# Attention tiles paired: one DMA transpose for two query tiles, another tile order, other places in the written order

## The chip, the cores and the metric

The kernel runs on one core of a Trainium2 chip. The metric is device time in microseconds (us), the median of several runs. The core has five engines with queues of their own: PE (matrix products), DVE (vector), ACT (scalar), POOL (GpSimd) and SP, which here only issues DMAs.

## The reference, cut to what matters

One transformer layer over x of 2 x 1024 tokens with 512 features: x = x + layernorm(attention(layernorm(x))), then x = x + layernorm(ffn(layernorm(x))). The attention has 32 heads with a compressed latent:

```
q      = rms_norm(x @ wq_a.T, q_norm_w) @ wq_b.T        # 32 heads of 128 + 64 (rotary)
kv     = x @ wkv_a.T                                    # latent of 64, rotary key of 64
kv_up  = rms_norm(kv[:64], kv_norm_w) @ wkv_b.T         # k_nope, v of each head
scores = (q_nope . k_nope + q_pe . k_pe) * scale        # causal mask
out    = softmax(scores) @ v ;  return out @ wo.T
```

The feed-forward part is silu(x @ w_gate) * (x @ w_up) @ w_down with a hidden width of 1376.

## The kernel before

Keys are folded into the queries' weights, so each head's query and key have 128 rows: 64 latent and 64 rotary. Both batches and 32 heads make 64 heads, worked one after the other. A head has eight query tiles of 128 queries; tile j sees (j + 1) x 128 keys, since the mask is causal. A job is one tile of one head, and there are 512 jobs (`NJ`), in the order of `TILES` within each head. Values are the latent itself, split into a high and a low fp16 half (`lat2`).

What a job goes through:

- scores (PE): fp32 split into high and low fp32r halves, three products (high x high, high x low, low x high) for each chunk of up to 512 keys, into one of four PSUM slots `s_ps` (`NS`, widths in banks in `SLOTS`). It waits for `q_split`, POOL's count of prepared 512-query halves, and for `p_low` of four jobs before.
- minimum (DVE, L1354): adds the mask and finds the row's extreme, whose value is read out by a second small instruction. exponential (ACT, L1152). split_high (ACT, L1159) and split_low (DVE, L1367): the probabilities as two fp16 halves in `pk`, a ring of `NPK` buffers.
- turn_probs (SP, L760): a DMA transpose from `pk` to `pt`, a ring of `NPT` buffers. It moves 2(j + 1) blocks of 128 x 128.
- values (PE, L972), once for two jobs: one matmul for each block into `o_ps`, whose column 128 is the sum of the row. invert_sums (DVE), outputs_norm (ACT, L1168, two instructions), outputs_add (POOL, L1561, once for four jobs), outputs_turn (PE, L980, four transposes once for four tiles of two heads), outputs_high (ACT), outputs_low (DVE).

Beside that run the queries of the next head in two halves (c = 0, 1): queries (PE, five matmuls of 512 columns into the bank `x_ps`), queries_raw (ACT, L1142, drains the bank), queries_swap (SP, L770, two DMAs that swap the rotary rows into `qs`), and queries_turn (POOL, L1531 to L1544, five instructions, the last of which writes q_low). Further, output (PE, 12 matmuls of 512 columns a head on average) multiplies four heads' outputs with folded weights, and fold_values prepares these in the first 32 heads. `x_ps` is one bank for queries, fold_values, outputs_turn and output, each of which waits until the one before it was drained.

Nothing is scheduled at run time. `attention_order` gives every piece of work a step on a common scale, one step for each job, and sorts them; each engine's program is the sorted list, cut to what that engine does. A step says only in which order an engine meets its work; the time follows from semaphores. `AFTER_SCORES`, `VALUES`, `AFTER_VALUES`, `TURN_STEPS`, `Q_STEPS` and the others are these distances: queries(n, c) stands at step 8(n - 1) + `Q_STEPS[c]`, values(u) at 2u + 1 + `VALUES`, and each list of AFTER is added to the step of the work that it is named for. Pieces with one step keep the order in which they were added, scores first. `prologue_order` does the same for the first stage (latents, folded weights), and `feed_forward_order` lets token and weight preparation advance by `pace` pieces beside each gate and up product. From `EARLY_START` on, pieces of the feed-forward part are laid between the last steps of attention.

Of the kernel before, what the change touches and what calls it, by code (L numbers as in the profile page):

```python
# [11 lines left out]
P = 128  # L12
# [23 lines left out]
NX, NA, NPK, NPT, NON = 4, 3, 4, 6, 8  # L36

SLOTS = (2, 1, 1, 2)
# [4 lines left out]
AFTER_SCORES = dict(minimum=0.86, exponential=0.73, split_high=1.39, split_low=2.35,  # L43
                    turn_probs=2.29)
VALUES = 6.15
AFTER_VALUES = dict(invert_sums=1.03, outputs_norm=0.4, outputs_add=2.09)
TURN_STEPS = (3.09, 3.21)
AFTER_TURN = dict(outputs_high=0.2, outputs_low=0.82)
Q_STEPS = (0.06, 2.46)
AFTER_QUERIES = dict(queries_raw=0.0, queries_swap=0.0, queries_turn=1.54)  # L50
O_STEPS = (3.53, 6.77)
AFTER_OUTPUT = dict(output_add=0.72, output_store=1.5)
FOLD_STEP = 1.04
AFTER_FOLD = dict(fold_high=0.0, fold_low=1.09, fold_store=1.5)
END_STEP = 7.5


AFTER_TILE = dict(x_load=-2.13, statistics=-0.35, deviation=-0.05, normalise=0.74, transpose_x=1.38,
                  x_high=1.56, x_low=2.15, project=3.23, squares=3.26, norm_keys=4.28, halves=5.02,
                  norm_queries=5.02, transpose_latents=5.91, latents_high=6.09, latents_low=6.62)  # L60
FOLD_FROM, FOLD_EVERY, LOAD_AFTER = 3.28, 2.2, 0.49
AFTER_WEIGHTS = dict(rotary=-0.29, weights_high=0.2, weights_low=0.84, fold_out=1.6)
FIRST_QUERIES = 0.18
TABLES_STEP = 6.94
EARLY_START = 1
# [12 lines left out]
TILES = [6, 1, 3, 7, 4, 0, 2, 5]  # L78
PLACE = [TILES.index(j) for j in range(JT)]
JOBS = [(n, j) for n in range(NHEADS) for j in TILES]  # L80
# [161 lines left out]
class Memory:  # L242
# [64 lines left out]
    def attention(self, ctx, sb, pb):  # L307
        self.m_in = sb(ctx, "m_in", [P, 2, GK, 2, DM], F32R)
        self.nbias = sb(ctx, "nbias", [P, 4])
        self.rinv = sb(ctx, "rinv", [P, NON])  # L310
        self.pk = sb(ctx, "pk", [P, NPK, 2 * SEQ], F16)
        self.pt = sb(ctx, "pt", [P, NPT, 2 * JT, P], F16)
        self.o_norm = sb(ctx, "o_norm", [P, NON, P])
        self.o_pair = sb(ctx, "o_pair", [P, 2, 4, P])
        self.ot_high = sb(ctx, "ot_high", [P, 2, GK, SEQ], F32R)
        self.ot_low = sb(ctx, "ot_low", [P, 2, GK, SEQ], F32R)
        self.acc = sb(ctx, "acc", [P, JT, DM])
        self.s_ps = [pb(ctx, f"s_ps{i}", n * CW) for i, n in enumerate(SLOTS)]
# [54 lines left out]
    def halves_of(self, i):  # L373

        width = (JOBS[i][1] + 1) * P
        return self.pk[:, i % NPK, 0:2 * width].rearrange("p (t h s) -> p t h s", h=2, s=P)
# [13 lines left out]
def prologue_order():  # L390
# [28 lines left out]
def attention_order(end):  # L419
# [15 lines left out]
    for u in range(NJ // 2):  # L435
        step = 2 * u + 1 + VALUES
# [132 lines left out]
def feed_forward_order():  # L569
# [117 lines left out]
def sync_program(e, M, S, D):  # L687
# [174 lines left out]
def tensor_program(e, M, S):  # L862
# [85 lines left out]
    def scores(i):  # L948
# [7 lines left out]
        for c, width in halves(j):  # L956
            keys = slice(b * SEQ + c, b * SEQ + c + width)
            ins = chain(e, s[:, c:c + width], three(M.q_high[:, r, q], M.q_low[:, r, q],
                                                M.k_high[:, keys], M.k_low[:, keys]))
        ins.then_inc(S.s_mm)  # L960

    def values(u):
        w.wait_ge(S.ident, 3)
        for i in (2 * u, 2 * u + 1):
            n, j = JOBS[i]
            b = HEADS[n][0]
            w.wait_ge(S.turned[i % NPK], DMA * (i // NPK + 1))
            if u:
                w.wait_ge(S.o_norm, u)
            blocks = range(2 * (j + 1))  # L970
# [109 lines left out]
def scalar_program(e, M, S):  # L1080
# [602 lines left out]
```

## Time and profile before

| | |
|---|---|
| median of 3 runs | 1831.28 us (1829.5 to 1832.15) |
| the profiled execution | 1834.6 us, span 1832.8 us |
| PE busy over the span | 1593.2 us (87%), 10720 matmuls |
| DVE, ACT, POOL busy | 1132.7, 1102.4, 951.7 us |
| mean granted TensorE clock | 0.96 |
| DMA transposes | 512, median 3.9 us from issue to landing |
| stages | latents to about 100 us, attention to about 1370, feed-forward to the end |

The span runs from the first to the last instruction; the execution's own time has some time around it. Engines' busy times overlap, so they don't add up to the span. In the profile L105 is the line of a helper that issues chains of matmuls; its groups are told apart by their tiles. A matmul's duration is longer than the distance to the next one's start, because they are pipelined. `SPq` rows are issues of DMAs on SP's queue.

### The profile page before, as it was taken

Reading aid. Unit: us, or ns where it says so; the run is one execution under the profiler, and the core shown is the slowest. Engines: PE = TensorE matmul, PEld = TensorE weight load, DVE = VectorE, ACT = ScalarE, POOL = GpSimd, SP = SyncE. Lnnn points to the kernel's source line nnn. Section 1 sums busy time; section 2 is a strip of 40 time slices with the busy share of each in tenths; the row PEclk is TensorE's granted clock in tenths of the full one; section 3 lists DMA queues with packets and bytes.
Section 4 is the critical chain, followed back from the end, with each engine's and each line's share of the span. In section 5 each row is a group of like instructions: output and inputs, shape, how many; then the busy total and the mean of one; then the engine's idle time right before and its main releaser. Section 6 shows DMA issues by size and latency. Waiting matters only on the chain. (4 is left out here: it accounts for less than half of the span.)

```text
span 1832.8 us, 30900 instructions
## 1 busy us (share of the span) xinstructions
PE 1593.2 (87%) x10720; PEld 1326.1 (72%) x10720; DVE 1132.7 (62%) x2548; ACT 1102.4 (60%) x2159; POOL 951.7 (52%) x911
## 2 busy tenths in 40 slices
PE   5877888989888888988989889888986889999986
PEld 5766776767777777777877777777775667888765
DVE  7856666767676767766767767676765453323355
ACT  5666776767676767767877767677762433312121
POOL 2655765666666656665766766666641232111132
PEclk9989999999999999999999999999997899999998
DMA  8668898989879988998889788888985500201022
GB/s 294 223 121 181 167 187 150 181 152 176 183 151 187 172 167 156 196 172 181 166 170 174 149 168 148 162 166 155 181 143 189 188 27 20 69 0 37 0 81 81
DMA packets 669291, 268.91 MB, mean 147 GB/s; under 512 B 616624, under 2 KB 627376, under 8 KB 666960
## 3 DMA queue, kind: packets, MB, share of 16 engines
q1 hardware_dynamic: 669136, 266.93, 68.8%
q8 instruction: 86, 1.41, 0.3%
q14 instruction: 69, 0.57, 0.1%
HBM read 69.70 MB, written 29.36 MB: 54 GB/s over the span
## 5 line engine op out<-in xcount | busy, mean ns | idle before, releaser
L1354 DVE CUSTOM_DVE_ANT_0 s_ps<-s_ps,far_sb 128x896 f32<-128x896 f32 (+7 forms) x512 | 388.2, 758 | 136.0 <-PE s_ps L105 135.3
L1367 DVE SCALAR_TENSOR_TENSOR pk<-s_ps,pk 128x896 f16<-128x896 f32 (+7 forms) x512 | 384.2, 750 | 115.4 <-ACT pk L1159 114.6
L1159 ACT ACTIVATE pk<-s_ps 128x896 f16<-128x896 f32 (+7 forms) x512 | 333.0, 650 | 91.4 <-DMA pt<-pk 79.9
L1152 ACT ACTIVATE s_ps<-s_ps,nbias 128x896 f32<-128x896 f32 (+7 forms) x512 | 367.5, 718 | 20.6 <-DVE nbias L1354 16.5
L105 PE MATMUL s_ps<-k_high,q_high 128*128 128x512 f32 (+3 forms) x768 | 289.6, 377 | 82.3 <-POOL q_low L1544 69.6
L972 PE MATMUL o_ps<-lat,pt 128*128 128x130 f16 x4608 | 317.6, 223 | 6.9 <-ACT o_norm L1168 3.6
L972 PEld LDWEIGHTS o_ps<-lat,pt 128*128 128x128 f16 x4608 | 271.7, 99 | 45.7 <-issue 31.5
L105 PE MATMUL s_ps<-k_low,q_high 128*128 128x512 f32 (+3 forms) x768 | 272.2, 354 | 0.0
L105 PE MATMUL s_ps<-k_high,q_low 128*128 128x512 f32 (+3 forms) x768 | 271.6, 354 | 0.0
L1531 POOL TENSOR_TENSOR qf<-q_raw,cos_q 128x512 f32<-128x512 f32 x128 | 163.5, 1278 | 207.5 <-ACT q_raw L1142 198.6
L1534 POOL TENSOR_TENSOR qs<-qs,sin_q 64x512 f32<-64x512 f32 x128 | 164.3, 1284 | 195.8 <-DMA qs<-q_raw 191.5
L105 PEld LDWEIGHTS s_ps<-k_high,q_high 128*128 128x128 f32 x768 | 148.7, 194 | 116.1 <-POOL q_low L1544 78.9
L1582 POOL TENSOR_TENSOR mid_low<-mid,mid_high 128x512 fp32r<-128x512 f32 (+1 forms) x44 | 57.9, 1315 | 327.5 <-ACT mid_high L1248 327.5
L1168 ACT ACTIVATE o_norm<-o_ps,rinv 128x128 f32<-128x128 f32 x512 | 159.6, 365 | 89.5 <-DVE rinv L1363 77.4
L105 PE MATMUL x_ps<-m_in,ot_high 128*128 128x512 f32 x492 | 163.2, 413 | 10.9 <-ACT q_raw L1142 7.6
L1537 POOL TENSOR_TENSOR qf<-qf,qs 64x512 f32<-64x512 f32 x128 | 164.2, 1283 | 10.0
L1544 POOL TENSOR_TENSOR q_low<-qf,q_high 128x512 fp32r<-128x512 f32 x128 | 163.3, 1276 | 10.2
L105 PEld LDWEIGHTS s_ps<-k_low,q_high 128*128 128x128 f32 x768 | 149.8, 195 | 20.7
L105 PEld LDWEIGHTS s_ps<-k_high,q_low 128*128 128x128 f32 x768 | 149.5, 195 | 16.8
L1142 ACT ACTIVATE q_raw<-x_ps 128x512 f32<-128x512 f32 x126 | 75.2, 597 | 140.8 <-PE x_ps L105 126.5
L105 PE MATMUL f_ps<-ft_high,w_high 128*128 128x512 f32 (+1 forms) x352 | 140.3, 398 | 6.8 <-DVE w_low L1447 4.4
L1461 DVE TENSOR_TENSOR mid<-f_ps,gate 128x512 f32<-128x512 f32 (+1 forms) x44 | 30.3, 690 | 180.7 <-PE f_ps L105 150.1
(134 smaller groups left out, 2703.0 us busy)
## 6 DMA issues: line engine op xcount, KB each, us to landing
weff_in<-weff SPq DMA_DIRECT2D x64, 256.0 KB, 3.1
qs<-q_raw SPq DMA_DIRECT2D x256, 64.0 KB, 2.2
weff<-weff_sb SPq DMA_DIRECT2D x8, 1024.0 KB, 4.9
wo_sb<-wo SPq DMA_DIRECT2D x16, 512.0 KB, 4.4
pt<-pk SPq DMA_TRANSPOSE x512, 3.9
m_fold<-m_in SPq DMA_DIRECT2D x8, 1024.0 KB, 5.3
m_in<-m_fold SPq DMA_DIRECT2D x8, 1024.0 KB, 6.3
xin<-x SPq DMA_DIRECT2D x16, 256.0 KB, 4.2
```

The source lines that it names most:

```text
L105: ins = e.matmul(out, stationary, moving, start=n == 0, stop=n == len(pairs) - 1)
L972: ins = e.matmul(M.o_ps[:, i % 2, :], M.pt[:, i % NPT, m, :], M.lat2[:, b * JT + m // 2, :], start=m == 0, stop=m == blocks[-1])
L1142: e.activation(M.raw[:, :], bank, ACT.Copy).then_inc(S.q_raw)
L1152: e.activation(M.scores_of(i), M.scores_of(i), ACT.Exp, bias=M.nbias[:, i % 4:i % 4 + 1], scale=-1.0).then_inc(S.exp)
L1159: e.activation(M.halves_of(i)[:, :, 0, :], M.tiles_of(i), ACT.Copy, scale=P_SCALE).then_inc(S.p_high)
L1168: ins = e.activation(M.o_norm[:, r, :], M.o_ps[:, side, 0:P], ACT.Copy, scale=M.rinv[:, r:r + 1])
L1354: e.tensor_tensor_reduce(out=s, in0=s, in1=M.far_sb[:, SEQ - width:SEQ], scale=1.0, scalar=3e38, op0=ALU.add, op1=ALU.min, accum_out=M.nbi ...
L1367: e.scalar_tensor_tensor(out=M.halves_of(i)[:, :, 1, :], in0=M.tiles_of(i), scalar=P_SCALE, in1=M.halves_of(i)[:, :, 0, :], op0=ALU.mult, ...
L1531: e.tensor_tensor(M.qf[:, :], M.raw[:, :], M.cos_q[:, col], ALU.mult).then_inc(S.q_cos)
L1534: e.tensor_tensor(M.qs[KVL:P, :], M.qs[KVL:P, :], M.sin_q[KVL:P, col], ALU.mult).then_inc(S.q_sin)
L1537: e.tensor_tensor(M.qf[KVL:P, :], M.qf[KVL:P, :], M.qs[KVL:P, :], ALU.add).then_inc(S.q_turned)
L1544: e.tensor_tensor(M.q_low[:, n % 2, col], M.qf[:, :], f32(M.q_high[:, n % 2, col]), ALU.subtract).then_inc(S.q_split)
```

## The change

- `TILES` goes from 6, 1, 3, 7, 4, 0, 2, 5 to 1, 6, 4, 3, 0, 7, 5, 2. Two neighbouring jobs (a pair u) now always have nine tiles of keys together, so 18 blocks with both halves. `SLOTS` becomes (1, 2, 2, 1) for it.
- `pk` and `pt` hold a pair in each buffer (2 x 9 blocks): three and four buffers of pairs, where four and six of single jobs were. `blocks_of` gives a job its part. One DMA transpose turns the pair, after p_low of its second job. split_high waits for the transpose of three pairs before.
- scores issues all products of q_high for all chunks, then all of q_low. The number of matmuls is the same.
- Nearly all distances of the written order change. The transposes have one of their own (`TURN_PROBS`), the tail's outputs are farther apart (`END_EVERY`), and the feed-forward pieces in the tail begin later (`EARLY_START` 6.94, one each 0.84 steps). `PACES` replaces 3, 4, 5 by 7, 3, 4.

```
-NX, NA, NPK, NPT, NON = 4, 3, 4, 6, 8
-SLOTS = (2, 1, 1, 2)
+NX, NA, NPK, NPT, NON = 4, 3, 3, 4, 8
+SLOTS = (1, 2, 2, 1)
...
-AFTER_SCORES = dict(minimum=0.86, exponential=0.73, split_high=1.39, split_low=2.35,
-                    turn_probs=2.29)
-VALUES = 6.15
-AFTER_VALUES = dict(invert_sums=1.03, outputs_norm=0.4, outputs_add=2.09)
-TURN_STEPS = (3.09, 3.21)
-AFTER_TURN = dict(outputs_high=0.2, outputs_low=0.82)
-Q_STEPS = (0.06, 2.46)
-AFTER_QUERIES = dict(queries_raw=0.0, queries_swap=0.0, queries_turn=1.54)
-O_STEPS = (3.53, 6.77)
-AFTER_OUTPUT = dict(output_add=0.72, output_store=1.5)
+AFTER_SCORES = dict(minimum=1.02, exponential=1.16, split_high=1.78, split_low=2.94)
+TURN_PROBS = 2.41
+VALUES = 6.09
+AFTER_VALUES = dict(invert_sums=1.31, outputs_norm=1.68, outputs_add=3.17)
+TURN_STEPS = (4.75, 4.72)
+AFTER_TURN = dict(outputs_high=0.0, outputs_low=0.96)
+Q_STEPS = (0.0, 2.66)
+AFTER_QUERIES = dict(queries_raw=0.69, queries_swap=0.03, queries_turn=1.93)
+O_STEPS = (4.97, 7.03)
+AFTER_OUTPUT = dict(output_add=0.36, output_store=1.5)
...
-END_STEP = 7.5
+END_STEP, END_EVERY = 9.71, 1.38
...
-EARLY_START = 1
+EARLY_START, EARLY_EVERY = 6.94, 0.84
+PACES = (7, 3, 4)
...
-TILES = [6, 1, 3, 7, 4, 0, 2, 5]
+TILES = (1, 6, 4, 3, 0, 7, 5, 2)
+PAIR = JT + 1
...
+def blocks_of(i):
+    tiles = JOBS[i][1] + 1
+    return slice(0, 2 * tiles) if i % 2 == 0 else slice(2 * (PAIR - tiles), 2 * PAIR)
...
-        self.pk = sb(ctx, "pk", [P, NPK, 2 * SEQ], F16)
-        self.pt = sb(ctx, "pt", [P, NPT, 2 * JT, P], F16)
+        self.pk = sb(ctx, "pk", [P, NPK, 2 * PAIR, P], F16)
+        self.pt = sb(ctx, "pt", [P, NPT, 2 * PAIR, P], F16)
...
-    def turn_probs(i):
-        j = JOBS[i][1]
-        w.wait_ge(S.p_low, i + 1)
-        if i >= NPT:
-            w.wait_ge(S.pv, (i - NPT) // 2 + 1)
-        e.dma_start_transpose(out=M.pt[:, i % NPT, 0:2 * (j + 1), :],
-                              in_=M.pk[:, i % NPK, 0:2 * (j + 1) * P]
-                              ).then_inc(S.turned[i % NPK], DMA)
+    def turn_probs(u):
+        w.wait_ge(S.p_low, 2 * u + 2)
+        if u >= NPT:
+            w.wait_ge(S.pv, u - NPT + 1)
+        e.dma_start_transpose(out=M.pt[:, u % NPT, :, :],
+                              in_=M.pk[:, u % NPK, :, :].rearrange("p t s -> p (t s)")
+                              ).then_inc(S.turned[u % NPK], DMA)
...
-            ins = chain(e, s[:, c:c + width], three(M.q_high[:, r, q], M.q_low[:, r, q],
-                                                M.k_high[:, keys], M.k_low[:, keys]))
+        for queries, sides in ((M.q_high, (M.k_high, M.k_low)), (M.q_low, (M.k_high,))):
+            for c, width in halves(j):
+                keys = slice(b * SEQ + c, b * SEQ + c + width)
+                for side in sides:
+                    ins = e.matmul(s[:, c:c + width], queries[:, r, q], side[:, keys],
+                                   start=queries is M.q_high and side is M.k_high,
+                                   stop=queries is M.q_low)
...
+        w.wait_ge(S.turned[u % NPK], DMA * (u // NPK + 1))
...
-        if i >= NPK:
-            w.wait_ge(S.turned[i % NPK], DMA * (i // NPK))
+        u = i // 2
+        if u >= NPK:
+            w.wait_ge(S.turned[u % NPK], DMA * (u // NPK))
```

## Rows read from the trace of the kernel before

**Rows 1.** Busy time by windows: us, busy us (instructions) of each engine, clock, DMA
```profile
...
110.00:1340.00 1230.00, 1079.55 (x8255) 908.62 (x8255) 830.98 (x1894) 885.43 (x1690) 792.27 (x736) 0.97 0.87 168
1340.00:1460.00 120.00, 90.60 (x491) 72.86 (x490) 71.93 (x145) 53.91 (x92) 29.28 (x27) 0.85 0.67 189
...
```

**Rows 2.** The tile view of s_ps: ns min/median/max, first and last start
```profile
...
L105 PE MATMUL s_ps<-k_high,q_high x768: 220/389/797, 92.5 to 1364.2; 128*128 128x512 f32 x128, 128*128 128x128 f32 x64
...
```

**Rows 3.** Waits of PE, 110 to 1340 us: us in total, times, longest
```profile
...
PE s_ps L105 <- POOL q_low L1544: 69.4, 52, 3.2
PE x_ps L980 <- POOL o_pair L1561: 30.0, 25, 3.7
PE x_ps L980 <- ACT q_raw L1142: 23.3, 30, 0.8
...
PE o_ps L972 <- DMA pt<-pk: 2.0, 3, 1.2
...
```

**Rows 4.** Timeline at a head's start: start, us, engine, line, operation, idle before
```profile
...
862.98 1.26 POOL L1544 TENSOR_TENSOR q_low<-qf,q_high 128x512 fp32r<-128x512 f32 x1
...
864.29 0.51 PE L105 MATMUL s_ps<-k_high,q_high 128*128 128x512 f32 x1 [1.40 <-POOL q_low L1544]
...
865.65 0.39 PE L105 MATMUL x_ps<-qa_high,weff_in 128*128 128x512 f32 x1
...
867.00 0.60 ACT L1142 ACTIVATE q_raw<-x_ps 128x512 f32<-128x512 f32 x1 [1.56 <-PE x_ps L105]
...
867.67 1.28 POOL L1531 TENSOR_TENSOR qf<-q_raw,cos_q 128x512 f32<-128x512 f32 x1 [2.53 <-ACT q_raw L1142]
...
```

**Rows 5.** Waits of POOL, 110 to 1340 us
```profile
...
POOL qs L1534 <- DMA qs<-q_raw: 189.8, 96, 6.8
...
```

**Rows 6.** Instruction groups, shapes apart: busy us, mean ns, idle before
```profile
...
L1354 DVE CUSTOM_DVE_ANT_0 s_ps<-s_ps,far_sb 128x1024 f32<-128x1024 f32 x64 | 78.6, 1228 | 27.0 <-PE s_ps L105 27.0
...
L1367 DVE SCALAR_TENSOR_TENSOR pk<-s_ps,pk 128x1024 f16<-128x1024 f32 x64 | 77.9, 1218 | 5.4 <-ACT pk L1159 5.3
...
L1354 DVE DVE_READ_ACCUMULATOR2_ANT nbias<- 128x1 f32 x512 | 72.2, 141 | 0.0
...
L1152 ACT ACTIVATE s_ps<-s_ps,nbias 128x1024 f32<-128x1024 f32 x64 | 69.8, 1090 | 0.2 <-DVE nbias L1354 0.2
...
L1159 ACT ACTIVATE pk<-s_ps 128x1024 f16<-128x1024 f32 x64 | 65.6, 1026 | 3.4 <-DMA pt<-pk 1.4
...
L1152 ACT ACTIVATE s_ps<-s_ps,nbias 128x128 f32<-128x128 f32 x64 | 22.1, 346 | 0.2 <-DVE nbias L1354 0.2
...
L1354 DVE CUSTOM_DVE_ANT_0 s_ps<-s_ps,far_sb 128x128 f32<-128x128 f32 x64 | 18.5, 290 | 0.0
L1367 DVE SCALAR_TENSOR_TENSOR pk<-s_ps,pk 128x128 f16<-128x128 f32 x64 | 18.5, 290 | 9.3 <-ACT pk L1159 9.2
L1159 ACT ACTIVATE pk<-s_ps 128x128 f16<-128x128 f32 x64 | 17.7, 277 | 13.5 <-DMA pt<-pk 11.7
...
```

**Rows 7.** The same view, output scaling and a weight load of the scores
```profile
...
L1168 ACT ACTIVATE o_norm<-o_ps,rinv 128x128 f32<-128x128 f32 x512 | 159.6, 365 | 89.5 <-DVE rinv L1363 77.4 <-issue 10.3
...
L105 PEld LDWEIGHTS s_ps<-k_low,q_high 128*128 128x128 f32 x768 | 149.8, 195 | 20.7
...
```

**Rows 8.** Line L760: the transpose of tile 1, of tile 7, landing of all
```profile
...
L760 SPq DMA_TRANSPOSE pt<-pk x1: 1258/1258/1258, 834.8 to 834.8; - x1
...
DMA to landing us min/median/max: 2.5/2.5/2.5
...
L760 SPq DMA_TRANSPOSE pt<-pk x1: 3067/3067/3067, 838.8 to 838.8; - x1
...
DMA to landing us min/median/max: 6.4/6.4/6.4
...
DMA to landing us min/median/max: 2.3/3.9/7.1
...
```

More of the change, by code:

```diff
@@ L51 @@
-O_STEPS = (3.53, 6.77)
-AFTER_OUTPUT = dict(output_add=0.72, output_store=1.5)
-FOLD_STEP = 1.04
-AFTER_FOLD = dict(fold_high=0.0, fold_low=1.09, fold_store=1.5)
-END_STEP = 7.5
[L58 to L61, printed above, removed]
@@ L62 @@
-AFTER_WEIGHTS = dict(rotary=-0.29, weights_high=0.2, weights_low=0.84, fold_out=1.6)
-FIRST_QUERIES = 0.18
+AFTER_SCORES = dict(minimum=1.02, exponential=1.16, split_high=1.78, split_low=2.94)
[7 more added lines that the diff above has]
+O_STEPS = (4.97, 7.03)
@@ new lines @@
+AFTER_OUTPUT = dict(output_add=0.36, output_store=1.5)
+FOLD_STEP = 1.07
+AFTER_FOLD = dict(fold_high=0.02, fold_low=1.08, fold_store=1.5)
+END_STEP, END_EVERY = 9.71, 1.38
+AFTER_TILE = dict(x_load=-2.13, statistics=-0.35, deviation=-0.05, normalise=0.81, transpose_x=1.12,
+                  x_high=1.65, x_low=2.42, project=3.04, squares=3.26, norm_keys=4.49, halves=4.87,
+                  norm_queries=5.21, transpose_latents=5.29, latents_high=6.13, latents_low=6.62)
+FOLD_FROM, FOLD_EVERY, LOAD_AFTER = 3.28, 2.2, 0.3
@@ L64 @@
+AFTER_WEIGHTS = dict(rotary=-0.26, weights_high=0.2, weights_low=0.61, fold_out=1.36)
+FIRST_QUERIES = 0.12
+AFTER_FIRST = dict(queries_raw=0.33, queries_swap=-0.67, queries_turn=1.22)
 TABLES_STEP = 6.94
-EARLY_START = 1
+EARLY_START, EARLY_EVERY = 6.94, 0.84
+PACES = (7, 3, 4)
 LN_EPS, RMS_EPS = 1e-5, 1e-6
@@ L373, in halves_of @@
     def halves_of(self, i):
-        width = (JOBS[i][1] + 1) * P
-        return self.pk[:, i % NPK, 0:2 * width].rearrange("p (t h s) -> p t h s", h=2, s=P)
+        return self.pk[:, i // 2 % NPK, blocks_of(i), :].rearrange("p (t h) s -> p t h s", h=2)
     def bank_of(self, g, j):
@@ L413, in prologue_order @@
         at(step, "queries", 0, c)
-        then(step, AFTER_QUERIES, 0, c)
+        then(step, AFTER_FIRST, 0, c)
     for _, _, turn in sorted(turns):
@@ L435, in attention_order @@
     for u in range(NJ // 2):
+        at(2 * u + 1 + TURN_PROBS, "turn_probs", u)
         step = 2 * u + 1 + VALUES
@@ L459, in attention_order @@
             else:
-                step = NJ + END_STEP + PLACE[j]
+                step = NJ + END_STEP + END_EVERY * PLACE[j]
             at(step, "output", g, j)
@@ L475, in attention_order @@
             at(step + 1, "values_load", p + 1)
-    for step in range(NJ + EARLY_START, int(max(turns)[0]) + 1):
+    step, over = NJ + EARLY_START, max(turns)[0]
+    while step < over:
         for turn in until_pause(end):
-            at(step + 0.9, *turn)
+            at(step, *turn)
+        step += EARLY_EVERY
     for _, _, turn in sorted(turns):
@@ L588, in feed_forward_order @@
         g, tb = BLOCKS[n] if n < len(BLOCKS) else (None, None)
-        pace = 0 if g is None else 3 if g >= 2 else 4 if tb else 5
+        pace = 0 if g is None else PACES[0] if g >= 2 else PACES[1] if tb else PACES[2]
         if g is not None:
@@ L955, in scores @@
             w.wait_ge(S.p_low, i - NS + 1)
-        for c, width in halves(j):
-            keys = slice(b * SEQ + c, b * SEQ + c + width)
-            ins = chain(e, s[:, c:c + width], three(M.q_high[:, r, q], M.q_low[:, r, q],
-                                                M.k_high[:, keys], M.k_low[:, keys]))
+        for queries, sides in ((M.q_high, (M.k_high, M.k_low)), (M.q_low, (M.k_high,))):
[5 more added lines that the diff above has]
+                                   stop=queries is M.q_low)
         ins.then_inc(S.s_mm)
@@ L963, in values @@
         w.wait_ge(S.ident, 3)
+        w.wait_ge(S.turned[u % NPK], DMA * (u // NPK + 1))
+        if u:
+            w.wait_ge(S.o_norm, u)
         for i in (2 * u, 2 * u + 1):
[L965 to L970, printed above, removed]
+            b = HEADS[JOBS[i][0]][0]
+            blocks = range(2 * PAIR)[blocks_of(i)]
             for m in blocks:
-                ins = e.matmul(M.o_ps[:, i % 2, :], M.pt[:, i % NPT, m, :],
-                               M.lat2[:, b * JT + m // 2, :], start=m == 0, stop=m == blocks[-1])
+                ins = e.matmul(M.o_ps[:, i % 2, :], M.pt[:, u % NPT, m, :],
+                               M.lat2[:, b * JT + (m - blocks[0]) // 2, :], start=m == blocks[0],
+                               stop=m == blocks[-1])
         ins.then_inc(S.pv)
```

## Prediction

> **What bounds the kernel now.** I first read the windows, to split the span into stages. [rows 1] gives the steady part of attention, 110 to 1340 us: PE is busy 1079.55 of 1230 us, ACT 885.43, DVE 830.98, POOL 792.27, and the DMA engines 0.87. The tile view [rows 2] dates the first score matmul at 92.5 us and the last at 1364.2: 64 heads in 1271.7 us, 19.87 us a head, 2.48 us for each of a head's eight steps. The window then holds 1230 / 19.87 = 61.9 heads, so PE works 17.4 us a head and stands for 150.45 us in all, 2.4 us a head; ACT works 14.3, DVE 13.4, POOL 12.8. No engine is full. PE is nearest, and a head can't be shorter than 17.4 us at the clock of this window. Then I read who PE waits for [rows 3]: q_low of POOL 69.4 us in 52 stalls, o_pair of POOL 30.0, and, before outputs_turn's transposes, ACT's drain of the single bank x_ps 23.3. That is 122.7 of the 150.45 us. The landing of transposed probabilities costs PE 2.0 us.
>
> The timeline of one head's start [rows 4] shows the loop behind the largest stall. PE starts tile 6 of the new head at 864.29, after 1.40 us idle, 0.05 us after POOL's q_low ends (862.98 + 1.26). Only behind these scores stand the query matmuls of the head after it (865.65), ACT drains them at 867.00, and POOL, idle for 2.53 us, begins at 867.67. Tile 6 needs both 512-token halves of the queries, so POOL's end gates PE, PE's queries gate POOL, and neither can run ahead. POOL also waits 189.8 us for the swapped halves from DMA [rows 5], whose issue stands in SP's queue between transposes.
>
> **The change, part by part.**
>
> *Tile order.* The head now begins with tile 1, which waits for the first half of the queries alone (`q_split` of 2n + 1). In the written order, queries(n+1, 0) stands at step 0.0, behind tile 1 and ahead of tile 6 at step 1. So PE computes them before it can be held by POOL's second half, and POOL finds q_raw ready when it finishes that half. The loop of [rows 4] is opened. POOL's own load, 12.8 us a head, fits into 17.4 with 4.6 to spare for swaps. I credit 60 of the 69.4 us; none is the lower bound, 69.4 the upper.
>
> *Steps of the output side.* outputs_turn(c0) stood at step 4.24 of its head, one step behind outputs_add (3.24), which in POOL's queue followed a query turn begun at 1.60. Now it is add 4.26, turn 5.84, the query turn ahead of it at 1.93. The other outputs_turn stood at 0.36, directly behind queries at 0.06 on the same bank; now 1.81 behind 0.0, while ACT's drain takes 0.60 [rows 4]. The 30.0 and 23.3 us should mostly go: I credit 45 of 53.3, with 0 and 53.3 as bounds.
>
> *What ACT and DVE allow.* The 105 us credited would give 19.87 - 105 / 61.9 = 18.2 us a head, and here the softmax passes come into play. In DVE's queue split_low of job i stands just ahead of minimum of job i+2 (2.35 and 2.86 before, 2.94 and 3.02 now), so the jobs of one parity form a loop of minimum, exponential, split_high, split_low. One 1024-wide tile costs 1.228 + 0.141 + 1.090 + 1.026 + 1.218 = 4.70 us and one 128-wide 0.290 + 0.141 + 0.346 + 0.277 + 0.290 = 1.34 [rows 6]; 0.48 us for each further 128 columns. Before, the longer loop had tiles 6, 3, 4, 2: 4 x 1.34 + 15 x 0.48 = 12.6 us a head. Now the odd jobs are 6, 3, 7, 2: 4 x 1.34 + 18 x 0.48 = 14.0. Sixteen handovers at 0.05 us add 0.8 in both. What is more, outputs_norm now stands at 2u + 1 + 6.09 + 1.68, in each head at steps 0.77, 2.77, 4.77, 6.77, between exponential (odd, 0.16) and split_high (0.78) of just these jobs, where before (1.55) it stood while DVE worked. Four pairs of 0.365 us [rows 7] add 2.9, and queries_raw (0.69) 0.6. The loop is 18.3 us a head. PE's 17.4 lies below it, so the loop is next. I take 18.5 us, with 0.2 for what it waits for others. The bounds are 17.4 (norms and drains slip beside it) and 19.87.
>
> *One transpose for two tiles.* The number falls from 512 to 256, the 128-column blocks stay 72 a head (4 x 18), so the DMA engines' work stays. SP's issue took 1.258 us at tile 1 (4 blocks) and 3.067 at tile 7 (16 blocks); these two landed 2.5 and 6.4 us after issue, and all 512 after 2.3 to 7.1, median 3.9 [rows 8]. By (6.4 - 2.5) / 12 = 0.33 us a block, 18 blocks would take 7.1 us; by the median 3.9 for the mean tile of 9 blocks, (3.9 - 2.5) / 5 = 0.28 a block gives 6.4. I take 6.4, the case nearest to a 16-block row, with 3.9 (blocks cost nothing more) and 7.1 as bounds. SP issues four at about 3 us in place of eight: no more than before. From the scores of the second job to values stand 6.09 steps, 14.1 us at 18.5 us a head. They must hold: the scores 1.36 us (864.29 to 865.65 in [rows 4]), 4.70 of passes and 6.4 of landing, 12.5 us, with 1.6 left for queues. The transposes now wait in SP's queue for p_low of the second job, at steps 1.41, 3.41, 5.41, 7.41; behind that of 7.41 stands the swap of the first query half (0.03), behind that of 1.41 the second's (2.69) and the next queries_load. POOL waits for these swaps, and its 4.6 us to spare cover about two such delays a head. So values cost nothing under this cover; without it each us late costs one us a pair, 4 a head, until the steps widen. Here a rule of the Trainium skill speaks against the change: "DMA: Bandwidth & Descriptors", Rules for kernel authors, says to issue a DMA early and wait on it late, and the first tile of a pair is now issued a job later. By that rule every pair would land late, and the time would be that of rival B below. The trace agrees so far only in that waits placed late are cheap (2.0 us on PE).
>
> *Buffers.* split_high waited on the transpose of four jobs before; now on that of three pairs before, five or six jobs back. The scores' slots stay four. Nothing on PE for it, below or above.
>
> *Stationary order.* Each of the 768 k_low,q_high matmuls has its weight load although k_high,q_high just before it used the same half of the queries [rows 7]. The loads aren't merged now, so putting more passes on one stationary merges none: 36 loads and 36 matmuls a head, cost 0. If it did merge some, PE would gain at most the load's 0.195 us at each of the six 128-column matmuls of a head, which are too short to hide one: 1.2 us a head of PE's time.
>
> *Prologue, tail and feed-forward.* The first scores wait for the weights' DMAs, not the queries; later outputs in the tail (END_STEP 9.71), later filler (6.94 for 1) and other paces move work among queues. PE stands 29.4 us in 1340 to 1460 [rows 1]. I take 0, with -10 to +10, a third of that stretch's idle time either way.
>
> **Sum.** 64 x (19.87 - 18.5) = 88 us off, against the 105 credited. The profiled execution took 1834.6 us (span 1832.8), 3.3 over the median 1831.28, so it gives 1746.6 and, at the median, **1743 us**.
>
> **The rivals.**
>
> *A, the softmax loop takes nearly all.* If outputs_norm waits for rinv inside the loop and outputs_high (about 0.6 every second head) with it, 18.3 grows past 19.3. For it: the norms' place. Against it: values stand 1.68 steps ahead. At 19.5 us a head: 24 us off, 1807. The swap remaining behind transposes in SP's queue (waits of 189.8 us) would give the same.
>
> *B, slower: values wait for the pair's landing.* The wait of q_low is replaced by one for pt. The path of scores, passes, queues and landing is fixed in us, the place of values in steps: period = 8 x path / 6.09. It decides from 6.09 x 2.48 = 15.1 us on: with 12.5 as above, queues of over 2.6 us. With landing at 7.1 and queues of 2.4, 15.6 us, the head is 20.5 us: 40 us more, 1871. For it: a loop at 18.3 leaves queues in front of each pass. Against: PE waited only 2.0 us on pt.
>
> *C, loads of a repeated stationary vanish after all.* PE's 17.4 us a head would fall by at most 1.2 to 16.2, but the softmax loop of 18.3 would hold the head, so only the 0.2 us of waits could go: 13 us beyond the forecast, 1730. [rows 7] speaks against it: the loads of a repeated half are all there. If they stay, the stationary order does nothing, and that is my forecast for it.
>
> *D, nothing is left:* POOL's stall is traded for SP's, period 19.87, 1831.
>
> **How the numbers follow.** Forecast 0.60 (18.1 to 19.1 us a head, 1718 to 1782), rival A 0.15, B 0.16, C 0.04, D 0.05. Low end: 17.8 us a head, 1699. High end: through rival A, 1826. Below it lies 0.04, above it B with 0.16. A measurement tells 0.2% (3.7 us) from no change. Faster: forecast, A, C, 0.79; same 0.05; slower 0.16.
>
> **What the profile after would show.** Right: PE's wait for q_low under 15 us, POOL's for q_raw under 60, 256 transposes, 768 loads of each kind, first-to-last score about 1184 us, and ACT or DVE's pk as PE's first releaser. Wrong in B: PE's o_ps waits on pt of over 60 us. Wrong in A: q_low gone, but s_ps waits on DVE pk over 80 us. A clock much below 0.97 would also spoil it.

## The result and the profile after

The changed kernel takes 1715.01 us, the median of 4 runs (1710.41 to 1718.1), against 1831.29 before. The ratio is 0.9364 with a 95% interval of 0.934 to 0.9388: 116 us or 6.4% faster. The profiled execution took 1718.1 us, with a span of 1716.3.

The tile view of the changed kernel answers to [rows 2], the window of its steady part (us, busy us of PE, weight loads, DVE, ACT, POOL, then clock and share of the DMA engines) to [rows 1]:

```profile
...
L973 PE MATMUL s_ps<-k_high,q_high x768: 220/388/776, 96.2 to 1266.0; 128*128 128x256 f32 x64, 128*128 128x128 f32 x64, 128*128 128x512 f32 x64
...
```

```profile
...
110.00:1220.00 1110.00, 1040.25 (x8111) 844.72 (x8112) 830.51 (x1864) 840.58 (x1664) 781.81 (x725) 0.99 0.92 183
...
```

The first score matmul starts 3.7 us later than before (96.2 for 92.5). From the first to the last it is 1169.8 us, 18.28 us a head for 19.87, so 101.9 us less. From the last score to the end of the span it is 450.3 us for 468.6, 18.3 us less. Together: -101.9 - 18.3 + 3.7 = -116.5, which is the difference of the spans. The window holds 1110 / 18.28 = 60.7 heads. PE works 17.1 us in each for 17.4 before, at a granted clock of 0.99 for 0.97, and stands 69.75 / 60.7 = 1.15 us for 2.4.

PE's waits in that window, to be read against [rows 3] (us in total, times, longest; the window is 110 us shorter):

```profile
...
PE o_ps L987 <- DMA pt<-pk: 37.4, 32, 3.3
PE x_ps L116 <- DVE ot_low L1391: 12.7, 29, 0.4
PE x_ps L996 <- DVE m_in L1398: 5.4, 8, 0.9
PE x_ps L996 <- POOL o_pair L1578: 4.2, 8, 0.6
...
PE s_ps L973 <- POOL q_low L1561: 1.6, 6, 0.3
...
```

The waits for q_low and o_pair, 69.4 and 30.0 us before, are 1.6 and 4.2, and the drain of q_raw is no longer in the list. The landing of a pair is now the first: 37.4 us for 2.0. POOL's waits, for [rows 5], and those of SP's queue:

```profile
...
POOL qs L1551 <- DMA qs<-q_raw: 209.7, 77, 4.5
POOL qf L1548 <- ACT q_raw L1158: 54.8, 53, 3.6
...
```

```profile
...
SPq L772 <- DVE pk L1384: 367.2, 204, 5.7
SPq L129 <- POOL qf L1554: 58.1, 47, 2.4
SPq L782 <- ACT q_raw L1158: 15.1, 16, 2.1
...
```

POOL still waits as long for its swap (209.7 us, 3.5 a head; it was 189.8, 3.1 a head). What it lost is the wait for q_raw: 54.8 us are left, where the same view of before had 188.3.

Two of the three rows of SP's queue are true idle time: the gaps between its instructions ahead of these are 54.0 and 15.8 us. The first is not. SP's own rows cover 975 of the 1110 us, so it can't stand 367.2 us for DVE. Set against the low half of its own second job, each of the 242 transposes of the window starts after it, 1.7 us later in the mean (median 1.6), and the gaps ahead of them add up to 22.0 us. The row counts the low halves of later jobs that end while a transpose is being issued. So a pair mostly waits for SP's queue, and SP seldom for a pair. One case from the timeline (start and duration in us), the pair of tiles 1 and 6, whose last low half ends at 712.16:

```profile
...
709.32 5.30 SPq L772 DMA_TRANSPOSE pt<-pk  x1
...
711.07 1.09 DVE L1384 SCALAR_TENSOR_TENSOR pk<-s_ps,pk 128x896 f16<-128x896 f32 x1 [0.40 <-ACT pk L1176]
...
714.71 1.17 SPq L782 DMA_DIRECT2D qs<-q_raw  x2
...
715.98 2.83 SPq L772 DMA_TRANSPOSE pt<-pk  x1
...
```

SP is still issuing the pair before and two swaps, and this pair's transpose starts 3.8 us after its data were there. The transposes of line L772, for [rows 8]:

```profile
...
L772 SPq DMA_TRANSPOSE pt<-pk x242: 2406/2867/6072, 110.9 to 1215.5; - x121
...
DMA to landing us min/median/max: 4.6/4.8/9.6
...
```

A pair of 18 blocks lands 4.8 us after its issue begins in the median (5.3 in the mean), and the issue holds SP's queue for 2.87 us.

The path of a pair can be read from the trace for 241 of the window's pairs. From the end of the second job's scores to its low half pass 5.8 us in the mean, then 1.7 until the transpose starts, 5.3 until it lands, and 1.5 us are left before values begin. In 27 cases values had to wait over 0.3 us for the landing. There the four are 6.2, 2.0, 7.0 and nothing: what is longer than in the others is above all the landing (7.0 us for 5.1), not the stand in SP's queue (2.0 for 1.7). Of the 16 pairs that were in flight together with a load of folded weights (`m_in<-m_fold`, 1 MB), 8 are among the 27, and their landing took 6.8 us in the mean. That the load delays them is a reading; no run tests it.

### The profile page after: what moved, and what is told of

Same layout as the page of the kernel before. It is cut to its first block, busy times and chain, and to the rows that moved or that the text cites. A ratio compares the mean times of both kernels' runs of the same rounds, so it can differ in the third digit from the quotient of the medians.

```text
span 1716.3 us, 30452 instructions
## 1 busy us (share of the span) xinstructions
PE 1572.2 (92%) x10720; PEld 1275.9 (74%) x10720; DVE 1147.7 (67%) x2548; ACT 1069.0 (62%) x2159; POOL 952.9 (56%) x911
## 4 chain that ended last, share of the span: by engine, by line
PE 56%; DMA 14%; DVE 11%; ACT 6%; POOL 6%; issue 4%; SPq 2%; POOLq 0%; ACTq 0%; DVEq 0%
PE f_ps L116 14%; PE s_ps L973 12%; PE x_ps L116 11%; DMA pt<-pk 10%; PE o_ps L987 9%; PE fd_ps L116 6%; DMA qs<-q_raw 3%; DVE pk L1384 3%; PE x_ps L996 2%; DVE s_ps L1371 1%; POOL q_low L1561 1%; POOL qf L1554 1%; POOL qs L1551 1%; SPq L772 1%; ACT ot_high L1194 1%
## 5 line engine op out<-in xcount | busy, mean ns | idle before, releaser
L1384 DVE SCALAR_TENSOR_TENSOR pk<-s_ps,pk 128x256 f16<-128x256 f32 (+7 forms) x512 | 383.7, 749 | 132.7 <-ACT pk L1176 132.4
L1168 ACT ACTIVATE s_ps<-s_ps,nbias 128x256 f32<-128x256 f32 (+7 forms) x512 | 371.3, 725 | 129.7 <-DVE nbias L1371 126.2
L1371 DVE CUSTOM_DVE_ANT_0 s_ps<-s_ps,far_sb 128x256 f32<-128x256 f32 (+7 forms) x512 | 388.4, 759 | 36.1 <-PE s_ps L973 30.9
L1176 ACT ACTIVATE pk<-s_ps 128x256 f16<-128x256 f32 (+7 forms) x512 | 339.6, 663 | 34.1 <-DMA pt<-pk 28.4
L987 PE MATMUL o_ps<-lat,pt 128*128 128x130 f16 x4608 | 312.0, 221 | 51.6 <-DMA pt<-pk 41.9
L973 PE MATMUL s_ps<-k_high,q_high 128*128 128x512 f32 (+3 forms) x768 | 283.6, 369 | 5.0 <-DVE k_low L1351 2.0
L973 PE MATMUL s_ps<-k_low,q_high 128*128 128x512 f32 (+3 forms) x768 | 257.1, 347 | 0.0
L973 PE MATMUL s_ps<-k_high,q_low 128*128 128x512 f32 (+3 forms) x768 | 224.3, 346 | 0.0
L973 PEld LDWEIGHTS s_ps<-k_high,q_low 128*128 128x128 f32 x768 | 135.4, 190 | 8.1
L116 PE MATMUL f_ps<-ft_low,w_high 128*128 128x512 f32 (+1 forms) x352 | 140.9, 400 | 0.0
```

Source lines behind the costliest of these rows:

```text
L116: ins = e.matmul(out, stationary, moving, start=n == 0, stop=n == len(pairs) - 1)
L973: ins = e.matmul(s[:, c:c + width], queries[:, r, q], side[:, keys], start=queries is M.q_high and side is M.k_high, stop=queries is M.q_low)
L987: ins = e.matmul(M.o_ps[:, i % 2, :], M.pt[:, u % NPT, m, :], M.lat2[:, b * JT + (m - blocks[0]) // 2, :], start=m == blocks[0], stop=m == ...
L1168: e.activation(M.scores_of(i), M.scores_of(i), ACT.Exp, bias=M.nbias[:, i % 4:i % 4 + 1], scale=-1.0).then_inc(S.exp)
L1176: e.activation(M.halves_of(i)[:, :, 0, :], M.tiles_of(i), ACT.Copy, scale=P_SCALE).then_inc(S.p_high)
L1371: e.tensor_tensor_reduce(out=s, in0=s, in1=M.far_sb[:, SEQ - width:SEQ], scale=1.0, scalar=3e38, op0=ALU.add, op1=ALU.min, accum_out=M.nbi ...
```

## The experiments

All times below are medians, each with the ratio to the kernel before on the same chip. "The pair" is the two tiles of one transpose.

### What opened the gain: the place of the query matmuls

**e2: the changed kernel with the next head's query matmuls back behind tile 6.** fold_values and its low half moved with them, since they share the bank.

```
-Q_STEPS = (0.0, 2.66)
+Q_STEPS = (1.0, 2.66)
-FOLD_STEP = 1.07
-AFTER_FOLD = dict(fold_high=0.02, fold_low=1.08, fold_store=1.5)
+FOLD_STEP = 1.75
+AFTER_FOLD = dict(fold_high=0.02, fold_low=0.9, fold_store=1.5)
```

> The changed kernel with the next head's first query matmuls placed behind tile 6 (step 1.0 for 0.0), where they again stand behind the wait for POOL's second half. Theory 1 (opening this loop is the main gain): PE's wait for q_low comes back, 40 to 70 us in the steady part, and the time is 1755 to 1785 us. Theory 2 (the merged transpose and SP's shorter queue are the gain): it stays within 10 us of 1715.

On ACT, queries_raw moves with them, behind an exponential, a split_high and an outputs_norm that it stood ahead of.

Measured: 1802.39 us, ratio 0.9819 (0.9762 to 0.9875), 87 us slower than the changed kernel. PE's, POOL's and SP's waits in it, same window:

```profile
...
PE o_ps L987 <- DMA pt<-pk: 55.1, 28, 7.2
PE s_ps L973 <- POOL q_low L1561: 34.4, 35, 1.6
...
```

```profile
...
POOL qf L1548 <- ACT q_raw L1158: 214.1, 56, 11.4
...
```

```profile
...
SPq L129 <- POOL qf L1554: 85.1, 56, 3.1
SPq L782 <- ACT q_raw L1158: 73.7, 62, 2.9
...
```

More than the expected range. The wait for q_low comes back with 34.4 us, less than expected, and POOL's for q_raw with 214.1 for 54.8. The rest shows as later landings, 55.1 us for 37.4. The swaps and the transposes share SP's queue, and SP stands 85.1 and 73.7 us ahead of the swaps, for 58.1 and 15.1; a pair's transpose starts 2.7 us after its data in the mean, for 1.7. I read it as the lateness of POOL and of queries_raw passed on to the pairs. Since both moved here, this run alone doesn't tell the place on PE from the place on ACT; e9 does.

**e9: the kernel before with one number changed.** It puts the query matmuls ahead of tile 6 on PE, without any other tile order. Raw, swap and turn move by the same 0.11 steps, but pass no neighbour on their engines.

```
-Q_STEPS = (0.06, 2.46)
+Q_STEPS = (-0.05, 2.46)
```

> The kernel before with one number changed: the next head's first query matmuls at step -0.05 for 0.06 (raw, swap and turn move with them), which puts them ahead of tile 6 on PE. If the place of these matmuls against POOL's wait is all, PE's wait for q_low (69 us in the steady part) goes, and the time is 1760 to 1790 us. If the tile order with a narrow first tile is needed as well, it stays within 10 us of 1831.

Measured: 1773.82 us, ratio 0.9654 (0.9617 to 0.9691): 60 us faster than the kernel before, by a move across one neighbour. PE's wait for q_low in the kernel before, in this shorter window, then PE's waits in e9:

```profile
...
PE s_ps L105 <- POOL q_low L1544: 61.0, 46, 3.2
...
```

```profile
...
PE x_ps L980 <- POOL o_pair L1561: 23.6, 21, 2.8
PE s_ps L105 <- POOL q_low L1544: 18.8, 18, 2.0
...
```

The wait for q_low falls from 61.0 to 18.8 us. The narrow first tile isn't needed to open the loop; that POOL's end no longer gates the matmuls that feed it is enough.

**e10: the kernel before with the tile order and the slots alone.**

```
-SLOTS = (2, 1, 1, 2)
+SLOTS = (1, 2, 2, 1)
-TILES = [6, 1, 3, 7, 4, 0, 2, 5]
+TILES = [1, 6, 4, 3, 0, 7, 5, 2]
```

> The kernel before with nothing but the new tile order (1, 6, 4, 3, 0, 7, 5, 2) and its slots (1, 2, 2, 1); old steps, one transpose for each job. Theory 1: this opens the loop by itself, PE's wait for q_low falls under 20 us and the time is 1760 to 1790 us; the stalls of outputs_turn (53 us) stay. Theory 2 (order and steps only work together): 1810 us or more.

Measured: 1841.96 us, ratio 1.0045 (1.0018 to 1.0072), slightly slower than before. Theory 2 holds for this half of the change. PE's waits say how:

```profile
...
PE x_ps L105 <- DVE acc L1390: 42.5, 42, 1.7
PE x_ps L980 <- POOL o_pair L1561: 29.7, 18, 2.5
PE x_ps L980 <- ACT q_raw L1142: 24.6, 27, 2.7
PE x_ps L105 <- ACT acc L1196: 12.5, 8, 2.8
PE o_ps L972 <- DMA pt<-pk: 11.2, 9, 2.9
...
PE s_ps L105 <- POOL q_low L1544: 0.6, 2, 0.4
...
```

The loop is open, q_low costs 0.6 us, and nothing is won. PE now comes early to the queries, and finds the bank x_ps still full of the output product of the step before (42.5 us for DVE's acc, 12.5 for ACT's), and the two stalls of outputs_turn (29.7 and 24.6) are about what they were (27.7 and 21.0 in this window). The two waits of the queries for the bank are new. So the queries don't reach POOL earlier after all: it waits 196.5 us for q_raw here, for 170.2 in the kernel before. In the changed kernel the output products, outputs_turn and the queries stand farther apart on the bank, and of these waits 12.7 us (ot_low), 5.4 (m_in) and 4.2 (o_pair) are left.

### What the merged transpose is worth

**e3: two transposes for each pair, both where the one stood.** Buffers and all else are the changed kernel's.

```
-        at(2 * u + 1 + TURN_PROBS, "turn_probs", u)
+        at(2 * u + 1 + TURN_PROBS, "turn_probs", 2 * u)
+        at(2 * u + 1 + TURN_PROBS, "turn_probs", 2 * u + 1)
...
+        e.dma_start_transpose(out=M.pt[:, u % NPT, blocks_of(i), :],
+                              in_=M.pk[:, u % NPK, blocks_of(i), :].rearrange("p t s -> p (t s)")
+                              ).then_inc(S.turned[u % NPK], DMA)
```

> The changed kernel with two transposes for each pair, both issued where the one stood, behind the low half of the second job; same buffers and order. Theory 1: merging is worth little, 1715 to 1730 us. Theory 2 (512 issues on SP and 512 fixed costs of a DMA were what held the kernel): most of the gain goes, 1780 us or more.

**e4: the same, but the first transpose is issued a job earlier**, at `2 * u + TURN_PROBS`, after its own low half.

```
-        at(2 * u + 1 + TURN_PROBS, "turn_probs", 2 * u)
+        at(2 * u + TURN_PROBS, "turn_probs", 2 * u)
         at(2 * u + 1 + TURN_PROBS, "turn_probs", 2 * u + 1)
```

> As before with two transposes a pair, but the first is issued a job earlier, as soon as its own low half is there. If late landing of the pair is what PE still waits for (37 us on pt), this gives it back: 1690 to 1710 us. If SP's queue is what makes the pair late (swaps and transposes behind one another), more issues and waits in it make it slower: 1720 to 1760 us.

Measured: e3 1769.84 us, ratio 0.963 (0.957 to 0.9689), 55 us slower than the changed kernel; e4 1720.09 us, ratio 0.9372 (0.9321 to 0.9422), the same as the changed kernel within the intervals. PE's wait on pt in e3, then in e4:

```profile
...
PE o_ps L989 <- DMA pt<-pk: 73.7, 56, 4.2
...
```

```profile
...
PE o_ps L989 <- DMA pt<-pk: 36.3, 34, 4.1
...
```

The means of a pair's way from its second low half on, read from the traces:

| | changed | e4 | e3 |
|---|---|---|---|
| until its (last) transpose starts, us | 1.7 | 2.8 | 3.9 |
| from there until all has landed, us | 5.3 | 4.1 | 4.2 |
| together | 7.0 | 7.0 | 8.1 |
| SP's rows, us a head | 16.1 | 17.2 | 17.2 |

So neither theory of e3 holds as it was put. With both issues behind the second low half the second of them starts late, and the pair lands 1.1 us later. Issued as each half is ready, two transposes are as good as one: the last one stands longer in SP's queue, but has fewer blocks and lands sooner. The merging saves 1.2 us a head of SP's time, and e4 shows that this time is worth nothing here: SP's rows fill 1042 of its 1110 us, more than the 996 of e3, and it is 50 us faster. What the merging doesn't do is make a pair land late: e4 has the same 36.3 us on pt.

### Products on one stationary half

**e1: the changed kernel with the old order of the score products.**

```
-        for queries, sides in ((M.q_high, (M.k_high, M.k_low)), (M.q_low, (M.k_high,))):
-            for c, width in halves(j):
...
+        for c, width in halves(j):
+            keys = slice(b * SEQ + c, b * SEQ + c + width)
+            ins = chain(e, s[:, c:c + width], three(M.q_high[:, r, q], M.q_low[:, r, q],
+                                                M.k_high[:, keys], M.k_low[:, keys]))
```

> The changed kernel with the score products in the old order (three for each chunk). If the number of weight loads is all that matters, and they stay 768 of each kind, the time is that of the changed kernel, 1715 us, within 0.2%. If more passes on one stationary half save time at the matmuls, it is slower by 10 to 20 us.

Measured: 1715.43 us, ratio 0.935 (0.9304 to 0.9397). It is worth nothing. The changed kernel has every load of a repeated half still in it (busy us, mean ns, idle before):

```profile
...
L973 PEld LDWEIGHTS s_ps<-k_low,q_high 128*128 128x128 f32 x768 | 146.6, 191 | 18.7
...
```

### The softmax loop of the prediction

**e5: outputs_norm moved out of the odd jobs' passes.**

```
-AFTER_VALUES = dict(invert_sums=1.31, outputs_norm=1.68, outputs_add=3.17)
+AFTER_VALUES = dict(invert_sums=1.31, outputs_norm=1.74, outputs_add=3.17)
```

> The changed kernel with outputs_norm at 1.74 for 1.68, which puts it behind split_high of the odd jobs in ACT's queue and so outside the passes of their loop. If the loop of the prediction (18.3 us a head, 2.9 of it these norms) is what holds a head at 18.28 us, the time falls by 20 us or more, to 1695 or below. If the loop doesn't bind, it stays within 8 us of 1715.

Measured: 1722.77 us, ratio 0.9408 (0.9387 to 0.9429), 8 us slower. DVE's waits in the changed kernel and in e5, then PE's in e5:

```profile
...
DVE pk L1384 <- ACT pk L1176: 127.4, 152, 3.5
...
DVE rinv L1380 <- PE o_ps L987: 16.7, 12, 4.2
...
```

```profile
...
DVE pk L1384 <- ACT pk L1176: 46.4, 97, 2.5
...
DVE rinv L1380 <- PE o_ps L987: 39.9, 105, 3.1
...
```

```profile
...
PE o_ps L987 <- ACT o_norm L1185: 28.5, 70, 1.3
PE o_ps L987 <- DMA pt<-pk: 27.7, 25, 3.4
...
```

The move did what it should inside the loop: DVE waits 81 us less for split_high. PE gains nothing from that and stands 28.5 us for o_norm instead (3.8 in the changed kernel), because values wait for the norm of the pair before. Since a new wait came in, this run doesn't by itself show that the loop had slack. It does show what the norms cost the loop: from the end of exponential to the start of split_high of the odd jobs pass 2.63 us a head in the changed kernel and 0.97 in e5, 1.7 us less, where the prediction counted 2.9.

**e6: all wide tiles in the odd jobs.**

```
-SLOTS = (1, 2, 2, 1)
+SLOTS = (1, 2, 1, 2)
-TILES = (1, 6, 4, 3, 0, 7, 5, 2)
+TILES = (1, 6, 3, 4, 0, 7, 2, 5)
```

> The changed kernel with tiles in the order 1, 6, 3, 4, 0, 7, 2, 5 (slots 1, 2, 1, 2): the same pairs, the first tile still narrow, but now all wide tiles are odd jobs (6, 4, 7, 5). The predicted sum for their loop is 4 x 1.34 + 22 x 0.48 + 0.8 + 2.9 + 0.6 = 20.2 us a head: if that sum is right, 1.9 us a head more, 1838 us. If the loop is looser than that sum, 1715 to 1750 us.

Measured: 1765.13 us, ratio 0.9636 (0.9615 to 0.9658). Its scores run from 95.0 to 1309.7 us, 18.98 us a head, where the sum of the prediction gave 20.2. A kernel can't run faster than a loop that binds it, so that sum is at least 1.2 us a head too long. The trace says where. The five passes of its odd jobs take 16.0 us a head, as predicted (15.9), and what stands between them 3.2, for 4.3 in the sum; between exponential and split_high it is 2.25 for 3.5. In the changed kernel the passes take 14.05 and what stands between them 4.3. As e6 gets by with 3.2, the changed kernel's loop had about 1.1 us a head of slack. Even here PE's waits name no softmax pass, though a late pass can also reach PE through the landing:

```profile
...
PE o_ps L987 <- ACT o_norm L1185: 42.0, 61, 1.5
PE x_ps L116 <- DVE ot_low L1391: 24.7, 28, 1.0
PE o_ps L987 <- DMA pt<-pk: 16.7, 15, 3.6
...
```

### Against the remaining wait

**e7: values and what follows them half a step later.**

```
-VALUES = 6.09
+VALUES = 6.59
```

> The changed kernel with values and all that follows them half a step later (VALUES 6.59 for 6.09). If the late landing of a pair is PE's main remaining wait and nothing else stands behind it, the waits on pt (37 us) go and the time is 1680 to 1700 us. If the landing waits are a sign of a queue that another loop sets, it stays within 8 us of 1715 and the wait appears elsewhere.

Measured: 1988.3 us, ratio 1.0865 (1.0832 to 1.0899), the miss of the study: 273 us slower than the changed kernel. PE's and DVE's waits:

```profile
...
PE o_ps L987 <- ACT o_norm L1185: 99.9, 104, 2.5
PE x_ps L996 <- POOL o_pair L1578: 67.5, 24, 4.3
PE x_ps L116 <- DVE ot_low L1391: 48.7, 46, 1.4
PE o_ps L987 <- DMA pt<-pk: 3.1, 2, 2.7
...
```

```profile
...
DVE rinv L1380 <- PE o_ps L987: 93.7, 115, 3.0
...
```

The wait on pt does go, to 3.1 us, but the head takes 22.5 us. The half step moves neither values nor invert_sums past a neighbour; it moves what follows them. In ACT's queue outputs_norm of pair u (2u + 9.27 for 8.77) falls behind split_high of job 2u + 7 (8.78) and exponential of job 2u + 8 (9.16). outputs_turn, outputs_high, outputs_low and outputs_add each pass a neighbour too. By this order a loop closes once a pair: that exponential needs the minimum of its job, which stands in DVE's queue behind invert_sums of pair u, and values of pair u + 1 need the norm of pair u. DVE waits 93.7 us for values (16.7 in the changed kernel), PE 99.9 us for o_norm (3.8) and 67.5 for o_pair (4.2). In e5 the norm passed split_high alone, for 8 us; how the 273 us divide among the other crossings no run tells.

**e11: the swaps issued from ACT's queue** instead of SP's, 1.14 steps behind the queries; the function moves from one engine's program to the other's.

```
-AFTER_QUERIES = dict(queries_raw=0.69, queries_swap=0.03, queries_turn=1.93)
+AFTER_QUERIES = dict(queries_raw=0.69, queries_swap=1.14, queries_turn=1.93)
-AFTER_FIRST = dict(queries_raw=0.33, queries_swap=-0.67, queries_turn=1.22)
+AFTER_FIRST = dict(queries_raw=0.33, queries_swap=0.34, queries_turn=1.22)
```

> The changed kernel with the query swaps issued from ACT's queue (at 1.14 steps behind the queries) instead of SP's. If SP's order (a swap that waits for POOL holds the pair's transpose behind it) makes the landing late, PE's wait on pt falls from 37 us to under 15 and the time is 1690 to 1705 us. If ACT loses as much by issuing four DMAs a head, 1715 to 1750 us.

Measured: 1780.2 us, ratio 0.9694 (0.9657 to 0.9731), 65 us slower than the changed kernel. PE's waits, and ACT's idle time ahead of exponential:

```profile
...
PE o_ps L979 <- ACT o_norm L1185: 58.5, 64, 3.0
PE o_ps L979 <- DMA pt<-pk: 20.6, 14, 3.4
...
```

```profile
...
ACT s_ps L1160 <- issue: 126.1, 77, 3.8
...
```

The second outcome, beyond its range. Without the swaps in SP's queue a transpose starts 0.2 us after its data in the mean, for 1.7, and the wait on pt falls to 20.6 us. The landing itself still takes 5.8 us in the mean. But ACT stands 126.1 us ahead of 77 exponentials in time that the profile gives to issue, where the swaps are, and PE waits 58.5 us for o_norm.

**e12: the swap of the second query half one place later in SP's queue**, behind the transpose of tiles 1 and 6.

```
-            then(step, AFTER_QUERIES, n, c)
+            then(step, {what: 0.78 if (what, c) == ("queries_swap", 1) else delay
+                        for what, delay in AFTER_QUERIES.items()}, n, c)
```

> The changed kernel with the swap of the second query half one place later in SP's queue, at step 3.44 for 2.69, behind the transpose of tiles 1 and 6 at 3.41. If this swap's wait for POOL (SP stands 58 us for it) is what makes that pair land late, PE's wait on pt falls from 37 us to under 20 and the time is 1698 to 1710 us. If POOL then gets its swap too late, the waits of POOL for qs grow past 260 us, q_low comes back on PE, and the time is 1720 us or more.

Measured: 1740.72 us, ratio 0.9493 (0.9464 to 0.9523), 26 us slower. PE's waits and POOL's:

```profile
...
PE s_ps L974 <- POOL q_low L1562: 47.2, 41, 2.4
PE o_ps L988 <- DMA pt<-pk: 12.3, 10, 2.1
...
```

```profile
...
POOL qs L1552 <- DMA qs<-q_raw: 276.2, 109, 6.7
...
```

Both halves of the expectation are seen at once: pt falls to 12.3 us, and q_low returns with 47.2 because POOL gets its swap late (276.2 us). SP's order of swap and transpose trades one of PE's waits for the other, and the changed kernel's order is the better of the two.

### The tail and the feed-forward part

**e8: the old numbers for the tail and the paces.**

```
-END_STEP, END_EVERY = 9.71, 1.38
+END_STEP, END_EVERY = 7.5, 1.0
-EARLY_START, EARLY_EVERY = 6.94, 0.84
+EARLY_START, EARLY_EVERY = 1.9, 1.0
-PACES = (7, 3, 4)
+PACES = (3, 4, 5)
```

> The changed kernel with the old places in the tail and the old paces of the feed-forward part (END_STEP 7.5, one a step; feed-forward pieces from 1.9 on, one a step; paces 3, 4, 5). The changed kernel takes 18 us less than the one before from the last score to the end. If these numbers are what gives it, 1728 to 1738 us; if attention's own end gives it, within 5 us of 1715.

Measured: 1734.5 us, ratio 0.9474 (0.9453 to 0.9495), 19 us slower than the changed kernel. Its scores take the same time (95.4 to 1262.7 us), and the stretch from the last score to the end is 470.0 us, as in the kernel before. The windows after the last score, of the kernel before and then of the changed one:

```profile
...
1364.20:1440.00 75.80, 52.12 (x244) 40.80 (x242) 44.73 (x85) 26.36 (x43) 15.09 (x13) 0.82 0.69 216
1440.00:1833.00 393.00, 361.32 (x1548) 286.77 (x1548) 157.04 (x268) 101.81 (x154) 82.31 (x63) 0.97 0.13 43
...
```

```profile
...
1266.00:1340.00 74.00, 57.75 (x285) 45.27 (x284) 47.01 (x89) 31.45 (x50) 16.94 (x14) 0.91 0.75 237
1340.00:1717.00 377.00, 351.88 (x1516) 279.31 (x1514) 155.70 (x262) 97.63 (x148) 80.71 (x61) 0.97 0.12 42
...
```

Over both windows PE's busy time differs by 3.8 us (413.4 and 409.6) and its idle time by 14.0 (55.4 and 41.4). About half of it is saved in the first of the two, where it falls from 23.7 to 16.3 us.

## Why the prediction was right, and where not

The time forecast was 1743 us, the measured one is 1715. It is 3 us below the 1718 to 1782 that the forecast gave its own mechanism.

**Tile order and queries.** Right in mechanism. 60 of 69.4 us were credited; 1.6 are left, and e9 gains 60 us by the place of the queries alone. The prediction tied it to the narrow first tile, and e9 shows that it isn't needed. It also took the credits as additive, and e10 shows that they aren't: with the order alone, 55 us of waits for the bank took the place of the one removed. So the new tile order gains only together with the new steps, as the change has them, while in the old order the queries' step gains alone.

**Output side.** 45 of 53.3 us were credited, and 4.2 are left, with 12.7 and 5.4 us of new waits for the same bank. Right in kind and nearly in size.

**What ACT and DVE allow.** This step failed. It said that the loop of odd jobs is next, at 18.3 us a head, "PE's 17.4 lies below it, so the loop is next". The measured 18.28 agrees with this number by luck. With wider odd tiles (e6) the kernel beats the sum by 1.2 us a head, without the norms between the passes (e5) nothing gets faster, and neither DVE's nor ACT's pk is among PE's releasers. The passes were right (14.05 for 14.0); the term that was wrong is what stands between them. The norms and the drain were put at 3.5 us a head and are 2.6 in the changed kernel and 2.25 in e6, and that this can shrink when the passes grow was left out. What PE waits for instead is the landing of pairs, 37.4 us. SP's queue has a part in it (e12, e11: with the swap behind, or gone from the queue, the wait falls to 12.3 and 20.6 us). In the cases where PE did wait, the landing itself was the longer term. No run removes the wait on pt without bringing another, so what would bound the kernel without it stays open.

**One transpose for two tiles.** The landing was put at 6.4 us and is 4.8 in the median, 5.3 in the mean; with the stand in SP's queue of 1.7 it comes to 7.0, of the 8.0 that the prediction had for both. The price of nothing holds (e4). The rule of the Trainium skill ("DMA: Bandwidth & Descriptors", Rules for kernel authors) to issue a DMA early and wait on it late would have made the single transpose a loss. Here two transposes gain 50 us by the early issue of the first (e4 for e3), as the rule says, but the early half gives nothing over the single one. That the wait on pt would stay small was wrong in size: 37.4 us, under the 60 that would have meant rival B. The median pair keeps its cover; single pairs cross rival B's point, those with late landings. e7 takes this wait away and costs far more, through what it moves along with values.

**Buffers and stationary order.** Both at nothing; e1 confirms the second. Rival C is excluded by it and by the loads that are all there.

**Prologue, tail and feed-forward.** Put at 0, with 10 us either way; measured 3.7 later at the start and 18.3 less at the end, the latter confirmed by e8. This is the largest mis-sized term: its idle time of 29.4 us stood in [rows 1], and the prediction shows no rows of what PE waits for there.

**Sum.** 88 us were forecast, all in attention. Attention gave 101.9, as the period was 18.28 for 18.5, and the rest gave 14.6. Not attributed by any run is how the gain left beside e9's and e8's, some 37 us, divides between the output side's steps, the clock and the tile order in their company. The clock's part is at most about 20 us, an estimate: PE's work fell from 17.4 to 17.1 us a head with the granted clock at 0.99 for 0.97, over 64 heads.

None of the runs beats the changed kernel.

## What to carry to other kernels

Look for a loop in which an engine's late result gates the very work that feeds it, and move the feeding work ahead of the wait: in the kernel before one number was worth 60 us. Expect stalls behind the removed one, on the same bank or queue, and move them in the same step, or nothing is won. In an order written by hand, a place just ahead of or behind a waiting neighbour matters more than a distance: half a step cost 273 us, though the piece that it was meant to move passed nothing. List what passes what on each engine before believing in the reason for a move. And check a wait that the profile gives to a DMA queue against the gaps between that queue's own rows: here one of 367.2 us was really 22.

## What the runs showed of the hardware

- The order of passes over a repeated stationary half changes nothing: every matmul keeps its weight load (768 of each kind), 1715.43 and 1715.01 us.
- A DMA transpose of 18 blocks of 128 x 128 in fp16 holds SP's queue for 2.87 us in the median and lands 4.8 us after its issue begins. In the kernel before, those of 4 blocks hold it 1.26 us and land after 2.6, those of 16 blocks 2.6 and 4.8 us, in the median.
- Two transposes of a pair, both issued behind the second low half, land 1.1 us later than one merged one in the mean (8.1 and 7.0 us after the data). With the first issued early they land no later (7.0).
- Issuing the swaps from ACT's queue leaves 126.1 us in front of ACT's exponentials in 1110 us, in 77 pieces, and the kernel takes 1780.2 us for 1715.
